# Two heads of a pair in the two row halves of the matmul array: a windowed attention stage changed in its scores, its exponentials and the way its row maxima travel

## The reference, cut to what matters

```python
def proj(W, b):
    y = jnp.einsum('bne,fe->bnf', x, W) + b
    return y.reshape(B, N, H, d).transpose(0, 2, 1, 3)      # H = 16, d = 16
q, k, v = proj(Wq, bq), proj(Wk, bk), proj(Wv, bv)
energy = jnp.einsum('bhqd,bhkd->bhqk', q, k)
out_of_window = jnp.abs(idx[:, None] - idx[None, :]) > WINDOW   # WINDOW = 128
energy = jnp.where(out_of_window, fmin, energy)
att = jax.nn.softmax(energy / jnp.sqrt(E), axis=-1)             # E = 256
out = jnp.einsum('bhqk,bhkd->bhqd', att, v)
return jnp.einsum('bne,fe->bnf', out.transpose(...).reshape(B, N, E), Wp) + bp
```

## Time and profile before

| | us |
|---|---|
| median of 3 runs | 1413.09 (1412.78 to 1414.12) |
| the profiled execution | 1405.96 |
| its span | 1404.1 |
| PE busy | 1337.1 (95%) |
| DVE busy | 697.5 (50%) |
| ACT busy | 465.7 (33%) |
| POOL busy | 448.4 (32%) |

### The profile page before, as it was taken

The page is one execution under the profiler, slowest core; times in us unless marked ns, Lnnn a source line. Parts: engine busy times, 40 slices in busy tenths (PEclk is TensorE's granted clock), DMA queues, the critical chain, the costliest instruction groups (busy, mean ns, idle before and its releaser), DMA issues.

```text
span 1404.1 us, 23272 instructions
## 1 busy us (share of the span) xinstructions
PE 1337.1 (95%) x7425; PEld 985.4 (70%) x7425; DVE 697.5 (50%) x2534; ACT 465.7 (33%) x939; POOL 448.4 (32%) x541
## 2 busy tenths in 40 slices
PE   7699999999999999999999999999998999999998
PEld 5366555667777777655666666666666789999998
DVE  5455447333333333345888888898879222210000
ACT  2121211112111211121576666766756512111111
POOL 2110000153222222161454544544423534443332
PEclk9899999999999999999999999999999999999999
DMA  9801100011122212123644645555432689999996
GB/s 326 293 24 37 46 0 1 15 57 61 61 62 64 64 61 61 49 78 101 168 135 132 185 115 150 165 143 152 139 116 77 247 314 340 339 329 345 340 339 216
DMA packets 89605, 208.77 MB, mean 149 GB/s; under 512 B 11118, under 2 KB 45296, under 8 KB 79505
## 3 DMA queue, kind: packets, MB, share of 16 engines
q1 hardware_dynamic: 73664, 172.19, 37.6%
q0 software_dynamic: 12096, 32.13, 7.6%
q10 hardware_dynamic: 3728, 2.97, 0.7%
HBM read 156.00 MB, written 52.17 MB: 148 GB/s over the span
## 4 chain that ended last, share of the span: by engine, by line
PE 81%; DVE 8%; issue 4%; SPq 3%; ACT 2%; DMA 2%; DVEq 0%; POOLq 0%; ACTq 0%
PE psum L807 12%; PE psum L976 10%; PE psum L986 10%; PE psum L672 9%; PE psum L786 7%; PE psum L683 6%; PE psum L833 4%; PE psum L880 4%; PE psum L904 3%; PE psum L855 3%; DVE work L1854 3%; PE psum L938 2%; PE psum L915 2%; PE psum L765 2%; PE psum L795 2%
## 5 line engine op out<-in xcount | busy, mean ns | idle before, releaser
L1854 DVE CUSTOM_DVE_ANT_0 work<-psum,mask 128x384 bf16<-128x384 f32 (+1 forms) x512 | 230.9, 485 | 56.8 <-PE psum L833 55.1
L807 PE MATMUL psum<-arena,work 128*128 x568 | 185.0, 468 | 0.5 <-issue 0.5
L833 PE MATMUL psum<-kz,qT 96*128 96x384 f32 (+1 forms) x512 | 166.4, 396 | 10.9 <-DVE small L1854 10.4
L1933 POOL DMA_INDIRECT work<-normed,token_of x71 | 67.5, 951 | 333.0 <-PE psum L765 206.1
L672 PE MATMUL psum<-arena 128*128 128x512 f32 x320 | 147.6, 600 | 0.0
L976 PEld LDWEIGHTS psum<-arena 128*128 128x128 f32 x1248 | 145.5, 192 | 2.4 <-issue 0.4
L976 PE MATMUL psum<-arena 128*128 128x128 f32 x1248 | 146.1, 275 | 0.0
L1212 ACT ACTIVATE arena<-psum 128x384 f32<-128x384 f32 x256 | 112.2, 494 | 91.3 <-PE psum L855 90.0
L986 PE MATMUL psum<-arena 128*128 128x256 f32 x624 | 141.0, 379 | 0.0
L807 PEld LDWEIGHTS psum<-arena,work 128*128 128x128 f32 x568 | 102.1, 189 | 51.2 <-issue 2.2
L1714 DVE TENSOR_TENSOR arena<-psum,arena 128x256 f32<-128x256 f32 x39 | 16.6, 425 | 241.2 <-PE psum L986 241.2
(11 more groups left out here) (239 smaller groups left out, 1973.5 us busy)
## 6 DMA issues: line engine op xcount, KB each, us to landing
arena<-in_w SPq DMA_DIRECT2D x78, 1024.0 KB, 7.4
strips<-hi SPq DMA_DIRECT2D x64, 256.0 KB
kz<-strips SPq DMA_DIRECT2D x64, 192.0 KB, 3.1
qT<-strips SPq DMA_DIRECT2D x32, 384.0 KB, 4.7
results<-work SPq DMA_DIRECT2D x71, 128.0 KB, 1.7
strips<-lo SPq DMA_DIRECT2D x32, 256.0 KB
normed<-work SPq DMA_DIRECT2D x14, 512.0 KB, 6.4
X<-in_x SPq DMA_DIRECT2D x8, 512.0 KB, 10.5
```

Source lines behind the costliest of these rows:

```text
L807: m = e.matmul(psum[:, pair[u], 0:INTER], xsT0[:, b % 2, c * P:(c + 1) * P], wu0[:, bass.ds(x, 1), c, u * INTER:(u + 1) * INTER], start=(c ...
L833: m = e.matmul(psum[:, bk, at:at + w], qT[0:ROWS_S, slot, half, i * P:(i + 1) * P], kz[slot][0:ROWS_S, hd, lo_key:hi_key], start=True, sto ...
L1854: e.tensor_tensor_reduce(masked[:, n % 2, 0:w], psum[:, bank_of["scores", u, i, hd], at:at + w], mask[:, P - off:P - off + w], 1.0, MASKED ...
L1933: e.indirect_dma_start(out=xs[:, b % 3, :], out_offset=None, in_=normed[l][0:n, :], in_offset=bass.IndirectOffsetOnAxis(ap=token_of[:, l, ...
```

## The change

The two heads of a pair are put into the two row halves of the array. Head 0 has rows 0 to 47 (its 48 rows) and 48, 49 (its maximum, in two parts); head 1 has rows 64 to 111 and 112, 113. `kz` is half as large: no zeros, one block for a pair. A scores matmul has 48 rows where it had 96, an again matmul 50 where it had 100; their numbers (512 each), their columns and their place in PE's order are the same.

- Every head now has its own bank, in narrow tiles too: scores take the ring of three by heads, and again uses bank 3 for the first and bank 4 for the second head of every pair, wide or narrow.
- One exponential serves two heads in all tiles: over banks 3 and 4, 2 x 384 or 2 x 256.
- [...] ACT makes one copy of 36 rows into `maxima_now`, and SP brings two rows at a time to their place, four transfers for each unit. `pe_again` waits for these.
- `sp_place` has four transfers of 48 rows for a unit where it had two of 48 and one of 96. The ones under the keys are two memsets for a slot, in place of two memsets and two selects.

```diff
-ROWS_S, ROWS_T = 2 * ROWS_H, 2 * ROWS_H + 4
+HALF, ROWS_T = P // 2, ROWS_H + 2
@@ emptied()
             if kind == "maxima":
-                return maxima_placed, G // 2 * (k[0] + 1)
+                return maxima_turned, k[0] + 1
@@ pe_scores
             for k in range(2):
-                hd = 2 * half + k
-                if k == 0 or w > 2 * P:
-                    bk = next_of(s_ring(u))
-                    fill(e, ("scores", u, i, hd), bk)
-                    at = 0
-                else:
-                    at = w
...
-                m = e.matmul(psum[:, bk, at:at + w], qT[0:ROWS_S, slot, half, i * P:(i + 1) * P],
-                             kz[slot][0:ROWS_S, hd, lo_key:hi_key], start=True, stop=True)
+                hd, rows = 2 * half + k, slice(HALF * k, HALF * k + ROWS_H)
+                bk = next_of(s_ring(u))
+                fill(e, ("scores", u, i, hd), bk)
+                e.matmul(psum[:, bk, 0:w], qT[rows, slot, half, i * P:(i + 1) * P], kz[slot][rows, half, lo_key:hi_key],
+                         start=True, stop=True).then_inc(bank_full[bk], 1)
@@ pe_again
-                e.wait_ge(maxima_placed, G // 2 * (u + 1))
+                e.wait_ge(maxima_placed, 16 * MOVED * (u + 1))
             for k in range(2):
-                hd = 2 * half + k
-                if w > 2 * P:
-                    bk, at = AGAIN[k], 0
-                else:
-                    bk, at = AGAIN[half], w * k
...
+                hd, rows = 2 * half + k, slice(HALF * k, HALF * k + ROWS_T)
+                fill(e, ("again", u, j, hd), AGAIN[k])
+                e.matmul(psum[:, AGAIN[k], 0:w], kz[slot][rows, half, j * P:(j + 1) * P], qT[rows, slot, half, lo_q:hi_q],
+                         start=True, stop=True).then_inc(bank_full[AGAIN[k]], 1)
@@ act_exp
+            hd = 2 * half
             for i in range(2):
...
+                e.wait_ge(*done["again", u, j, hd + i])
+            e.activation(pT(u, j)[:, hd:hd + 2, 0:w], psum[:, AGAIN[0]:AGAIN[1] + 1, 0:w], ACT.Exp,
+                         scale=1.0 / E ** 0.5).then_inc(p_exped, 1)
@@ act_place_maxima becomes act_turn_maxima
-            for half in range(G // 2):
-                e.activation(qT[ROWS_S:ROWS_T, u % SLOTS, half, :], psum[32 * half:32 * half + G, bank_of["maxima", u], :],
-                             ACT.Copy).then_inc(maxima_placed, 1)
+            e.activation(maxima_now[0:32 + G, :], psum[0:32 + G, bank_of["maxima", u], :], ACT.Copy).then_inc(maxima_turned, 1)
@@ new on SP, at step 4u + 5, ahead of sp_place and sp_keep of that step
+        def sp_place_maxima(e, u):
+            if u >= SLOTS:
+                e.wait_ge(*done["again", u - SLOTS, TPB - 1, G - 1])
+            e.wait_ge(maxima_turned, u + 1)
+            for q in range(G // 2):
+                for k in range(2):
+                    e.dma_start(qT[HALF * k + ROWS_H:HALF * k + ROWS_T, u % SLOTS, q, :].bitcast(F32),
+                                maxima_now[32 * q + 2 * k:32 * q + 2 * k + 2, :].bitcast(F32)).then_inc(maxima_placed, 16)
```

More of the change, by code:

```diff
@@ L217, in over @@
             return nc.alloc_sbuf_tensor_at(name, shape, dt, offset=arena_at + 4 * word)
-        kz = [over(f"kz{i}", at, [P, G, N], F32R) for i, at in enumerate((21760, 23808, 25856, 0))]
+        kz = [over(f"kz{i}", at, [P, G // 2, N], F32R) for i, at in enumerate((21760, 23808, 25856, 0))]
+        maxima_now = over("maxima_now", 1024, [P, N], F32R)
         qT = over("qT", 2048, [P, SLOTS, G // 2, N], F32R)
@@ L501, in qk_number @@
             return 4 * b + 2 * c + i
-        PLACED, KEPT = 3, 3
+        PLACED, KEPT, MOVED = 4, 3, G
         H_RING = ((2, 3), (4, 5))
@@ L518, in exps_before @@
         def exps_before(u, j, hd):
-            wide = [window(n)[1] - window(n)[0] > 2 * P for n in range(TPB)]
-            per = [G if w else G // 2 for w in wide]
-            return u * sum(per) + sum(per[:j]) + (hd if j < TPB and wide[j] else hd // 2)
+            return G // 2 * (u * TPB + j) + hd // 2
         def m_ring(s):
@@ L843, in pe_again @@
             if j == 0 and half == 0:
-                e.wait_ge(maxima_placed, G // 2 * (u + 1))
+                e.wait_ge(maxima_placed, 16 * MOVED * (u + 1))
             for k in range(2):
-                hd = 2 * half + k
-                if w > 2 * P:
-                    bk, at = AGAIN[k], 0
-                else:
-                    bk, at = AGAIN[half], w * k
-                if k == 0 or w > 2 * P:
-                    fill(e, ("again", u, j, hd), bk)
-                else:
-                    bank_of["again", u, j, hd], done["again", u, j, hd] = bk, done["again", u, j, hd - 1]
-                m = e.matmul(psum[:, bk, at:at + w], kz[slot][0:ROWS_T, hd, j * P:(j + 1) * P],
-                             qT[0:ROWS_T, slot, half, lo_q:hi_q], start=True, stop=True)
-                if k == 1 or w > 2 * P:
-                    m.then_inc(bank_full[bk], 1)
+                hd, rows = 2 * half + k, slice(HALF * k, HALF * k + ROWS_T)
+                fill(e, ("again", u, j, hd), AGAIN[k])
+                e.matmul(psum[:, AGAIN[k], 0:w], kz[slot][rows, half, j * P:(j + 1) * P], qT[rows, slot, half, lo_q:hi_q],
+                         start=True, stop=True).then_inc(bank_full[AGAIN[k]], 1)
         def pe_maxima(e, u, ring):
@@ L1849, in dve_mask @@
             w, off, n = hi_key - lo_key, i * P - lo_key, (u * TPB + i) * G + hd
-            at = w * (hd % 2) if w <= 2 * P else 0
             if n >= 2:
@@ L1854, in dve_mask @@
             e.tensor_tensor_reduce(
-                masked[:, n % 2, 0:w], psum[:, bank_of["scores", u, i, hd], at:at + w], mask[:, P - off:P - off + w], 1.0,
+                masked[:, n % 2, 0:w], psum[:, bank_of["scores", u, i, hd], 0:w], mask[:, P - off:P - off + w], 1.0,
                 MASKED, ALU.add, ALU.max, mx[:, b % 2, i, G * g + hd:G * g + hd + 1]).then_inc(mx_made, 1)
@@ L1968, in pool_key_pads @@
                 e.wait_ge(*done["q0", B - 1])
[L1969 to L1977 removed]
+            for k in range(2):
+                e.memset(kz[i][HALF * k + 32:HALF * (k + 1), :, :].bitcast(F32), 1.0).then_inc(key_pads_made, 1)
+            e.wait_ge(key_pads_made, 2 * (i + 1))
         def pool_value_pads(e):
@@ L2145, in _ @@
             for s in range(FIRST_STEP, LAST_STEP):
+                for u, _ in unit(s, 5, 1):
+                    sp_place_maxima(e, u)
                 for first in (-5, -4):
```

51 lines of the change are left out of this document (14 added, 37 removed).

## The result

The kernel with the change takes 1502.2 us (1501.1 to 1505.2, four runs) where the kernel before took 1413.6 beside it: 1.063 times as long (95% interval 1.061 to 1.065). Slower was forecast, but +24 us and at most 1470; it is +89. The profiled execution took 1501.12 us.

The account below looks back on a forecast made before the run. PE was taken to set the attention's pace mostly, DVE close behind (48.5 us a batch as floor). Terms +36 - 25 + 16 - 12 + 5 + 4 = +24 us on 1413 gave 1437 us; range 1390 to 1470.

Parts of the forecast that it names:

- row halves and changes of shape: PE's scores and again in the attention: shorter pairs save 25 us on the path, switches of tile shape cost 36.
- transfers and copy: Maxima in the attention: waiting for SP's transfers costs 4 us, the ACT copy that goes saves 12.
- banks of the scores and of again: PE's waits in the attention for banks: 5 us for scores and 16 us for again.
- Banks of the scores: Narrow pairs need two of the ring's three banks, so PE meets DVE's masks sooner: +5 us.
- Banks of again: In narrow steps the second pair waits for the first's one exponential: 2.0 us a batch, +16 us; wide tiles little changed.
- The clock: Engines in the attention were read as all at the full granted clock; no term was given for a change.
- the sign: Whole kernel: slower, by +24 us; chance of slower 0.66.
- the changes of shape: On PE, 285 more switches between 128 and 64 rows at 0.19 us each: 54 us, 36 on the path.
- the pairs: Scores and again on PE: two loads one behind the other, 0.22 us a pair, saving 38 us, 25 on the path.
- The first rival: Attention: halves and loads run side by side, -50 us, and waits lie beside DVE's work; 1387 us, chance 0.25.
- The transfers: Maxima on SP for every second unit: four issues of about 0.4 us, again late by 0.5 us a batch, +4 us.
- the rival of late maxima: Two rows queue behind the place's 768 KB and half the units wait 2.5 us: +60, 1473 us, chance 0.09.

Follow-up runs that it names:

- the padded kernel: The kernel before, keys still padded and all array rows used, given parts of the change but no row halves; with all three parts 1490.6 us.
- one_exp: The kernel before with again using banks 3 and 4 for the two heads of every pair and one exponential serving both; 1465.1 us.
- two_exp: The kernel before with again using banks 3 and 4 in every step, but an exponential and a bank's release for each head; 1423.9 us.
- filled: The kernel after with one more unread matmul ahead of the second half's scores in every fourth attention step; 1513.2 us.
- values_first: The kernel after with TensorE's values of a unit issued ahead of the second half's scores of the same step; 1491.8 us.
- no_transfer: The kernel before with the scores' banks and one exponential for two heads, the maxima still copied by ScalarE; ratio 1.064–1.067, +92 us.
- by_transfer: The kernel before with one ACT copy of the maxima into a buffer and four transfers of two rows; 1430.6 us.
- own_exps: The kernel after with an exponential and a bank's release for each head in place of one for two; 1495.2 us.

## Why the prediction failed

Its sum by groups, and what the runs give for each: row halves and changes of shape -25 + 36 = +11, measured +12; transfers and copy +4 - 12 = -8, measured -16 beside the rest; banks of the scores and of again 5 + 16 = +21, measured +92 in the padded kernel. Together 24 and 88. The step that failed is the last.

**Banks of the scores.** "Wide scores waited 4.4 us on PE for a mask, narrow ones 0.3 [...] the difference for 32 units is +5 us, which I take." The step carried a wait over from the wide tiles by its length, and missed twice. The waits for masks grew to 36.9 us in the stage, from 10.4, where 5 more were forecast. And behind the wait in the narrow/narrow step stand the unit's values, PE's longest independent work there, with DVE behind in its own. In the padded kernel the banks cost 54 us alone and 27 as the last part added; with the values ahead of the wait they cost 8. The rule to name what is queued behind the waiting instruction was kept for the transfers and skipped here.

**Banks of again.** The wait itself was forecast nearly right: pair, exponential of 0.60, next pair, 0.35 us later than before in a narrow/narrow step; in one_exp PE waits 0.53 us there, at 810.27. It was counted for narrow tiles alone, 2.0 us a batch; "in wide tiles little changes" was wrong, since there too the second pair now waits for the joint exponential instead of the first head's own (20.5 us of waits in one_exp, 3.0 in two_exp). That one takes 0.81 us (0.80 was forecast), after:

```profile
L1191 ACT ACTIVATE arena<-psum 128x768 f32<-128x768 f32 x97 | 78.5, 810 | 106.3 <-PE psum L838 101.7 <-issue 0.6
L1191 ACT ACTIVATE arena<-psum 128x512 f32<-128x512 f32 x96 | 57.1, 594 | 81.5 <-PE psum L838 80.8 <-issue 0.7
```

Of the 51 us that this part costs alone, 39 go to the joint exponential, wide and narrow together.

**The clock, which had no term.** The forecast read "all at the full granted clock" in the earlier trace rows and took that as given. After, TensorE's pieces of the chain within the half-clock stretches add up to 99.5 us between 690 and 1180; before there are none. Had they run at full clock they would have taken about half (the values, 4.38 against 2.29), so up to some 50 of the 84 us lost in the stage are slow running rather than waiting. This is an estimate from the rows; no run holds the waits and gives the clock back, and filled, meant to, didn't. On the values alone it is 79 us of chain for 24 units against 2.29 each: 24 us. The estimate may be too high: values_first has 44 us less at half clock than the change and gains 9. Half clock and loss don't rise together exactly: no_transfer loses more than the whole change with 99 us at half clock against 147.

**Right:** the sign, though by another cause; that the stage's end moves the end of the kernel; the changes of shape, 0.19 in and 0.19 out forecast, 0.20 measured both ways. The Trainium skill's page "TensorEngine Tiling (Array Packing)" (Tiling Modes, Key Properties), where changing the mode drains the engine, agrees for the changes between 128 and 64 rows.

**Right by two errors:** the pairs. Loads one behind the other, 0.22 us a pair, was wrong; 0.12 and 0.17 is full overlap. The Trainium skill's page "TensorE: Matmul & The Clock Gate" (Part 3, measured speedup) had a packed group at about the time of one matmul, and this trace agrees: 0.12 us a pair, where two took 0.24. The first rival's condition (a wide pair under 0.20) held, yet its 1387 us did not come, for its other condition, that the waits lie beside DVE's work, did not hold. By these pairs -50 + 36 = -14 was due, and +12 came. In the chain the pairs freed little, 76 to 72 us, while the line behind the way back to all rows (L885, before L904) went from 9.9% of 336 to 11.8% of 396 us, 33 to 47; its rows carry half clock too, so the 26 us are not parted further.

**The transfers.** Four issues were put at 1.6 us on SP; by the median of 0.60 us each they take 2.4, and here they take 3.06:

```profile
815.03 3.06 SPq L2059 DMA_DIRECT2D qT<-maxima_now  x4
```

In the changed kernel the rival of late maxima was no danger: 4.3 us of PE's waits after, and moving them ahead changed nothing. In by_transfer it was nearer: 18.5 us in 13 waits, up to 2.9 us, the size that the rival named.

**Left open.** Whether the scores' banks can be given back with the row halves in place; no run has that, so the banks' price is shown in the padded kernel alone. Why the exponential's 27 us in the padded kernel become 7 to 9 in own_exps (which keeps banks 3 and 4 and gives each back on its own) isn't told apart. What makes the clock fall in some stretches with a wait and not in others stays open, and its 50 us stay an estimate. No version run beats the kernel before.

## What to carry to other kernels

Count banks as carefully as instructions: an edit that gives each head its own bank, or one instruction that holds two banks, sets how far the producer may run ahead, and its price depends on the work queued behind the wait, not on the wait's own length alone. Where TensorE sets the pace at full clock, read the granted clock behind new waits as well: here a wait of 1.2 us was followed by values at half speed, and by the estimate up to half of the loss lay there, though waits of 1.43 us had left the clock up before. Parts that only remove slack don't add; price each both alone and as the last one added.

## What the hardware showed beyond that

Two row halves with 48 or 50 rows and 128 columns each run fully side by side, loads included: 0.12 us a pair against 0.24 in narrow tiles, 0.17 against 0.35 in wide ones. After the change TensorE's clock fell to its lower level 20 times between 690 and 1180 us, as behind the wait of 1.24 us that ends at 857.66; before it, waits of 1.43 us (one ends at 769.32) left the clock at the upper level from 670 to 1069 us. A transfer of two rows of 2 KB from one part of the on-chip memory to another held SP's queue for 0.60 us at the median (0.56 to 1.51, 128 of them), as long as the issue of a strip beside it (0.62 us).
